# Second held part of the adjacency, a new order of the degree sums, and groups turned together with their sources

## The reference, cut to what matters

```python
# layer 0: two graph convolutions over the same matrix
A = adj + eye(n); d = rsqrt(A.sum(axis=1)); An = d[:, None] * A * d[None, :]
out = An @ (relu(An @ (x @ W1) + b1) @ W2) + b2
x = layernorm(x + out)
# layer 1: K = 2 heads of attention masked by (adj > 0) | eye
x_norm = ln(x, g1, b1)
h = x_norm @ ff0_w[i].T                      # for each head i
e = leaky_relu((h @ attn_w[i, :c])[:, None] + (h @ attn_w[i, c:])[None, :])
att = ln(softmax(where(mask, e, NEG), axis=1) @ h + x, g2, b2)
h_next += elu(att @ ff1_w[i].T) / K
x = layernorm(x + h_next)
```

## Time and profile before

| | us |
|---|---|
| median of 3 runs | 1012.15 (1011.77 to 1013.4) |
| the profiled execution | 1014.17 |
| its span, first to last instruction | 1011.5 |
| TensorE busy (matmuls) | 962.6 |
| VectorE busy | 729.5 |
| ScalarE busy | 485.6 |
| GpSimd busy | 231.9 |
| mean granted clock of TensorE | 0.985 |

### The profile page before, as it was taken

The page is one execution under the profiler, slowest core; times in us unless marked ns, Lnnn a source line. Parts: engine busy times, 40 slices in busy tenths (PEclk is TensorE's granted clock), DMA queues, the critical chain, the costliest instruction groups (busy, mean ns, idle before and its releaser), DMA issues. The chain is left out here.

```text
span 1011.5 us, 9279 instructions
## 1 busy us (share of the span) xinstructions
PE 962.6 (95%) x2491; PEld 455.4 (45%) x2492; DVE 729.5 (72%) x1289; ACT 485.6 (48%) x756; POOL 231.9 (23%) x226
## 2 busy tenths in 40 slices
PE   4888999999999999999999999999999999999993
PEld 3333344444644444444655454444444444444541
DVE  4977777765645434427878777888779899888977
ACT  3344433221200000000088768778677888978774
POOL 0322223233157000005600001000049501010013
PEclk9899999999999999999999999999999999999997
DMA  9999999999399999992322122223213233323211
GB/s 362 415 419 418 417 416 416 414 417 387 149 357 370 383 391 386 388 371 111 115 74 84 62 94 73 94 64 103 68 57 104 76 103 94 104 63 95 93 53 41
DMA packets 71378, 220.08 MB, mean 218 GB/s; under 512 B 5351, under 2 KB 44839, under 8 KB 61223
## 3 DMA queue, kind: packets, MB, share of 16 engines
q1 hardware_dynamic: 67360, 205.87, 54.1%
q10 hardware_dynamic: 3974, 13.73, 3.3%
HBM read 199.63 MB, written 19.96 MB: 217 GB/s over the span
## 5 line engine op out<-in xcount | busy, mean ns | idle before, releaser
L1502 PE MATMUL ps<-T,Yw 128*128 128x512 f32 x1024 | 444.5, 593 | 3.1 <-DVE T L1178 2.5
L1502 PE MATMUL ps<-colbuf,stat 128*128 128x512 f32 x800 | 349.2, 595 | 0.0
L1178 DVE SCALAR_TENSOR_TENSOR T<-T,mring 128x2048 f32<-128x2048 f32 x125 | 286.1, 2290 | 67.5 <-ACT T L692 66.6
L692 ACT ACTIVATE T<-Rrow,small,ratio 128x1024 f32<-128x1024 f32 x250 | 294.8, 1231 | 62.2 <-PE ps L1502 61.9
L1502 PEld LDWEIGHTS ps<-T,Yw 128*128 128x128 f32 x1024 | 194.0, 190 | 239.7 <-issue 231.7
L1502 PEld LDWEIGHTS ps<-colbuf,stat 128*128 128x128 f32 x800 | 152.5, 191 | 191.1 <-issue 190.9
L1008 DVE TENSOR_SCALAR mtile<-colbuf 128x4096 uint8<-128x4096 f32 x28 | 65.9, 2355 | 81.4 <-DMA mask<-mtile 81.4
L611 ACT ACTIVATE W<-W 128x1024 f32<-128x1024 f32 (+13 forms) x57 | 61.7, 1082 | 72.4 <-DMA W<-in_adj 71.5
L539 POOL TENSOR_SCALAR rs<-sumsq 128x4 f32<-128x4 f32 x14 | 15.9, 1138 | 309.7 <-ACT squares L739 309.7
L629 ACT ACTIVATE stat<-xw_g 128x128 f32 x20 | 6.2, 309 | 158.8 <-DVE mtile L1011 76.8
L485 POOL PARTITION_ALL_REDUCE Rrow<-W x32 | 36.1, 1127 | 164.2 <-DVE W L902 139.7
(11 more groups left out here) (203 smaller groups left out, 727.1 us busy)
## 6 DMA issues: line engine op xcount, KB each, us to landing
colbuf<-in_adjT SPq DMA_DIRECT2D x48, 1024.0 KB, 15.7
colbuf<-in_adjT SPq DMA_DIRECT2D x24, 2048.0 KB, 10.5
mring<-mask SPq DMA_DIRECT2D x128, 256.0 KB, 2.7
mask<-mtile ACTq DMA_DIRECT2D x26, 512.0 KB, 10.9
colbuf<-in_adjT SPq DMA_DIRECT2D x16, 768.0 KB, 15.5
W<-in_adjT SPq DMA_DIRECT2D x4, 2048.0 KB, 11.0
W<-in_adj SPq DMA_DIRECT2D x12, 512.0 KB, 12.3
Rrow<-s_src SPq DMA_DIRECT2D x9, 512.0 KB, 4.2
```

What stands on the lines that cost most here:

```text
L692: last = act.activation(T[:, c % TS, j, :], Rrow[:, g % 2, :], ACT.Relu, scale=ratio[:, c * JB + j:c * JB + j + 1], bias=small[:, 8:9])
L1178: v.scalar_tensor_tensor(out=tile, in0=tile, scalar=1.0, in1=mring[:, c % TS, :, :].rearrange("p b n -> p (b n)"), op0=ALU.add, op1=ALU.mu ...
L1502: return pe.matmul(*args, skip_group_check=True, **kw)
```

## The change

A second held part `side` (rows 4 to 15 of column blocks 4 and 5, 12 x 256 columns) lies in memory that is free at that time: the upper half of the row of 1/d and the buffer of source rows. It is loaded ahead of row 2. Rows 4 and 5 are then read from column 2048 on as well, and the column loads of blocks 4 to 15 leave out 256 columns more; TensorE's second group becomes two matmuls for them. Corner and side are summed by halving adds. The own sum of block b+1 is formed behind `diag` of block b, from tiles b-1 and b, and the long sum (now `scalar_tensor_tensor`) comes after it. The constant 1 of the diagonal goes into two later steps in place of L910. In the turn, groups 2 to 7 are multiplied by `turner`, the identity with the four source columns beside it, instead of being transposed; their last two blocks go into the bank of the group two before. Groups 0 and 1 keep the transposition and `sources`. ScalarE normalises and copies the source columns; GpSimd computes the combined scale `comb`; seven products z instead of eight stand ahead of the attention.

```diff
+    SB, SR = CB + 2, CR - CB
...
-        corner_part = Rrow[:, 0, 0:CB * P]
+        corner_part = Rrow[:, 1, 4 * P:8 * P]
+        side = [dinv_row[:, N // 2:N].rearrange("p (j n) -> p j n", j=CR // 2), Rrow[:, 0, :].rearrange("p (j n) -> p j n", j=CR // 4)]
+        side_part = Rrow[:, 1, 4 * P:6 * P]
...
         def row_parts(b):
 
-            from_block = CR if b < CB else b
+            from_block = CR if b < SB else b
...
             if b < CR:
-                return slice(CB * P, N // 2), slice(N // 2, N)
+                return slice((CB if b < CB else SB) * P, N // 2), slice(N // 2, N)
...
-        Z_FIRST, Z_BANKS, Z_WAITING = 4, 4, 8
+        Z_FIRST, Z_BANKS, Z_WAITING = 4, 3, 7
...
+                if b == 2:
+                    for part, landed, lo, hi in zip(side, side_loaded, (CB, CR - CB), (CR - CB, CR)):
+                        sp.dma_start(part, corner_cols[:, lo:hi, CB * P:SB * P]).then_inc(landed, 16)
...
+                if b == B // 2:
+                    pool.wait_ge(pe_block, COL_CREDIT + (CR - CB))
...
-                pool.tensor_tensor(rstd[:, group(k)], rstd[:, group(k)], half[:, group(k)], ALU.pow).then_inc(scale_ready, 1)
-
-            def scale_again(k):
-                pool.wait_ge(scale_ready, k + 1)
+                pstep(pool.tensor_tensor(rstd[:, group(k)], rstd[:, group(k)], half[:, group(k)], ALU.pow))
+                pool.wait_ge(means_ready, k + 1)
+                pool.tensor_tensor(shift[:, group(k)], neg_mean[:, group(k)], rstd[:, group(k)], ALU.mult).then_inc(scale_ready, 1)
+
+            def scale_both(k):
+
+                pool.wait_ge(moments_ready, k + 1)
                 own = group(k)
-                r = r2[:, own]
...
-
-            for k in range(NG):
+                r = comb[:, own]
+                pstep(pool.tensor_scalar(r, mv[:, own, 1], 1.0 + LN_EPS, 0.0, ALU.mult, ALU.add))
+                pstep(pool.tensor_tensor(r, r, eps_both[:, own], ALU.add))
+                pool.tensor_tensor(r, r, half[:, own], ALU.pow).then_inc(comb_ready, 1)
+
+            for k in range(NG - 1):
                 scale_rows(k)
-                scale_again(k)
+                scale_both(k)
+            scale_both(NG - 1)
+            scale_rows(NG - 1)
...
+            def copy_sources(k):
+                act.wait_ge(stats_ready, k + 1)
+                if k >= WHOLE:
+                    for i, at in enumerate((k, k - 2)):
+                        last = act.activation(raw_st[:, k * BPG + 2 * i:k * BPG + 2 * i + 2, :],
+                                              ps[:, at, 0:2 * TW].rearrange("p (b n) -> p b n", n=TW)[:, :, P:TW], ACT.Copy)
+                    last.then_inc(raw_st_ready, 1)
+
+            def copy_first_sources(k):
+                act.wait_ge(st_done, k + 1)
+                act.activation(raw_st[:, group(k), :], ps[:, k, OWN_ST:GW].rearrange("p (b m) -> p b m", m=2 * K), ACT.Copy)\
+                    .then_inc(raw_st_ready, 1)
+
+            def normalise(k):
+                act.wait_ge(scale_ready, k + 1)
+                for b in range(k * BPG, (k + 1) * BPG):
+                    last = act.activation(x1[:, b, :], turned(b), ACT.Identity, scale=rstd[:, b:b + 1], bias=shift[:, b:b + 1])
+                last.then_inc(x1_ready, 1)
+
+            for k in range(NG - 1):
...
+                copy_sources(k)
+                normalise(k)
+                if k < WHOLE:
+                    copy_first_sources(k)
+            copy_sources(NG - 1)
...
+            read_z(2)
+            normalise(NG - 1)
+            for r in range(3, Z_FIRST):
                 read_z(r)
...
+            def own_sums(b):
+
+                own = cols(b)
+                tiles = {CB: (b - 2, b - 1), CB + 1: (b - 2,)}.get(b, (b - 2, b - 1))
...
+                for n, tile in enumerate(tiles):
...
+                    v.tensor_tensor(colacc[:, own], colacc[:, own], colbuf[:, tile % RING, own], ALU.add)\
+                        .then_inc(own_step if b < SB or n == 0 else colown_done, 1)
+                if b < SB:
+                    v.wait_ge(own_step, steps + len(tiles))
+                    v.tensor_tensor(colacc[:, own], colacc[:, own], side_part[:, cols(b - CB)], ALU.add).then_inc(colown_done, 1)
+
             def add_rest(b):
 
-                before, rest = (b - 1) % RING, slice(max(b + 1, CB) * P, N)
-                if b < CB:
+                before, rest = (b - 1) % RING, slice(max(b + 2, CB) * P, N)
+                if b <= CB:
                     v.wait_ge(near_loaded[before], 16 * ((b - 1) // RING + 1))
                 if b <= HB2:
                     v.wait_ge(col_loaded[before], 16 * ((b - 1) // RING + 1))
                 if b == 1:
                     v.tensor_copy(colacc[:, rest], colbuf[:, before, rest]).then_inc(colacc_done, 1)
                 else:
-                    v.tensor_tensor(colacc[:, rest], colacc[:, rest], colbuf[:, before, rest], ALU.add).then_inc(colacc_done, 1)
-
-            def over_corner(out, rows, columns, done):
-                v.tensor_reduce(out, corner[:, rows, columns].rearrange("p j n -> p n j"), AX_X, ALU.add).then_inc(done, 1)
-
-            def corner_sums(b):
-
-                own = cols(b)
-                over_corner(colacc[:, own], slice(CR // CP, CR), own, corner_summed)
-                v.wait_ge(corner_summed, b + 2)
-                v.tensor_tensor(colacc[:, own], colacc[:, own], corner_part[:, own], ALU.add).then_inc(colown_done, 1)
+                    v.scalar_tensor_tensor(out=colacc[:, rest], in0=colbuf[:, before, rest], scalar=1.0, in1=colacc[:, rest],
+                                           op0=ALU.mult, op1=ALU.add).then_inc(colacc_done, 1)
+
+            CW = CB * P
+
+            def halve(scratch, k, out):
+
+                row0, wide = k * (CR // CP), CR // CP // 2
+                a = corner[:, row0:row0 + wide, :].rearrange("p j n -> p (j n)")
+                b = corner[:, row0 + wide:row0 + 2 * wide, :].rearrange("p j n -> p (j n)")
+                v.tensor_tensor(scratch[:, 0:4 * CW], a, b, ALU.add).then_inc(corner_summed, 1)
...
+                v.tensor_tensor(scratch[:, 0:2 * CW], scratch[:, 0:2 * CW], scratch[:, 2 * CW:4 * CW], ALU.add)\
+                    .then_inc(corner_summed, 1)
...
+                v.tensor_tensor(out, scratch[:, 0:CW], scratch[:, CW:2 * CW], ALU.add).then_inc(corner_summed, 1)
...
+
+            def side_sums():
+
+                scratch, wide = dinv_row[:, CB * P:CR * P], (SB - CB) * P
+                half = wide * (CR - CB) // 3
+                whole = side[0].rearrange("p j n -> p (j n)")
+                v.wait_ge(side_loaded[0], 16)
+                v.tensor_tensor(scratch[:, 0:half], whole[:, 0:half], whole[:, half:2 * half], ALU.add).then_inc(side_summed, 1)
+                v.wait_ge(side_loaded[1], 16)
+                v.wait_ge(side_summed, 1)
+                v.tensor_tensor(scratch[:, 0:half], scratch[:, 0:half], side[1].rearrange("p j n -> p (j n)"), ALU.add)\
+                    .then_inc(side_summed, 1)
...
-            over_corner(corner_part[:, :], slice(0, CR // CP), slice(0, CB * P), corner_summed)
+            halve(dinv_row[:, 0:N // 2], 0, corner_part)
             v.wait_ge(xw_done, NG)
             v.wait_ge(corner_loaded[1], 16)
-            corner_sums(0)
+            halve(colacc[:, N // 2:N], 1, colacc[:, 0:CW])
+            for b in range(CB):
+                v.tensor_tensor(colacc[:, cols(b)], colacc[:, cols(b)], corner_part[:, cols(b)], ALU.add).then_inc(colown_done, 1)
             for b in range(B):
                 u = b % RING
...
-                    v.wait_ge(colacc_done, b - 1)
-                    v.tensor_tensor(colacc[:, own], colacc[:, own], colbuf[:, before, own], ALU.add).then_inc(colown_done, 1)
-                elif b + 1 < CB:
-                    corner_sums(b + 1)
                 v.wait_ge(colrow_ready, b + 1)
                 v.tensor_tensor(colown[:, :], colrow[:, b % 2, :], ident[:, :], ALU.mult).then_inc(colpart_step, 1)
-                v.wait_ge(colpart_step, 3 * b + 1)
+                v.wait_ge(colpart_step, 2 * b + 1)
                 v.tensor_reduce(colpart[:, :], colown[:, :], AX_X, ALU.add).then_inc(colpart_step, 1)
-                v.wait_ge(colpart_step, 3 * b + 2)
-                v.tensor_scalar(colpart[:, :], colpart[:, :], 1.0, None, ALU.add).then_inc(colpart_step, 1)
-                if 1 <= b <= HB2:
-                    add_rest(b)
-                v.wait_ge(colpart_step, 3 * b + 3)
+                v.wait_ge(colpart_step, 2 * b + 2)
...
-                if HB2 < b < B - 1:
+                if b + 2 == CB:
+                    side_sums()
+                if CB <= b + 1 < B:
+                    own_sums(b + 1)
+                if 1 <= b < B - 2:
                     add_rest(b)
...
+                v.wait_ge(moments_ready, k + 1)
+                v.tensor_scalar(neg_mean[:, group(k)], mv[:, group(k), 0], -1.0, None, ALU.mult).then_inc(means_ready, 1)
...
+
```

(84 more changed lines are left out.)

131 lines of the change are left out of this document (69 added, 62 removed).

## The result

The changed kernel takes 1016.51 us (median of 7 runs, 1015.52 to 1018.34) against 1013.4 for the kernel before beside it (7 runs, 1011.77 to 1014.58): ratio 1.0036, 95% interval 1.0025 to 1.0048, so it is slower, by some 3.7 us, where 2.1 were forecast. Its profiled execution took 1015.83 us, span 1013.9.

The account below looks back on a forecast made before the run. VectorE's chain was taken as the degree stage's bound, DMA a close second, TensorE's work the turn's. Stage +3.7 and turn -1.6 gave +2.1 us: 1014.3 for the median, range 1003 to 1018.

Parts of the forecast that it names:

- part 1: Degree stage order: GpSimd's reduction, asked for just after the long sum begins, is blocked; 8.46 us a block, 0.1 more.
- once its reading is over, a sum doesn't hurt it: Degree stage: a reduction begun 0.54 us before long sum L876 still took 1.07 us.
- R1: Rival, degree stage: the reduction passes beside the long sum, blocks 7.0 us until DMA rules; 1004.5 us, chance 0.33.
- the pair L556 and L1178: GpSimd's L556 took 2.48 us (median 0.45) beside VectorE's three-operand L1178; taken as evidence that the reduction is blocked.
- part 2: Held columns, early blocks: 1.57 MB more up to row 3, 3.8 us at 418 GB/s; block 4 2.5 us late.
- The side adds: VectorE before block 3: four adds of 1024, 1024, 512 and 256 columns, 3.7 us with steps.
- the corner: Start of the degree stage: corner halved by adds, 4.3 us where L879 took 7.15; first `stat` within 0.5, taken as 0.
- The sum of the stage: Degree stage, blocked: 2.5 + 11 blocks x 0.08 + 0.3 for blocks 15 to 17 = +3.7 us; bounds +1.5 and +6.
- The turn: Turn of the groups: TensorE net -2.1, `highest` no longer waits, gref about 2.4 earlier; -1.6 us, bounds -2.5 and +2.
- R3: Rival, turn: bank waits on ScalarE stall TensorE two or three times by about 2.5 us; 1019.3 us, chance 0.10.
- R2: Rival: reduction blocked but early blocks cost nothing, stage even and the turn pays; 1010.5 us, chance 0.10.

Follow-up runs that it names:

- the first run: The changed kernel with the long sums written with two operands again: 1016.76 us, ratio 1.0036 to the kernel before.
- the turn alone: Degree stage of the kernel before, the rest as in the changed kernel, so only the turn is new: 1011.19 us, ratio 0.9984 to the kernel before.

## Why the prediction was nearly right

- *The mechanism, reduction blocked by the long sum* (part 1): right to 0.1 us. 8.46 us a block was forecast, 8.52 (blocks 4 to 5) and 8.46 (5 to 6) were measured; eleven blocks lose 0.7 where 11 x 0.08 = 0.9 was said. That three operands change nothing was shown by the first run. That "once its reading is over, a sum doesn't hurt it" holds for the row it was read from, but not for the copy of block 1: in the trace before, a reduction begun 0.54 us ahead of that copy (L874, 31.77) took 2.80 us.
- *R1* fell, and the reason given for keeping it high (the excluding rows are of other operations) was no reason: the pair L556 and L1178 was a good model. What R1 would have given is approached by moving the request: blocks of 6.9 to 7 us, then waits for tiles, 0.9938 to 0.9946 x 1012.15 = 1005.9 to 1006.7, against its 1004.5.
- *The early blocks* (part 2) are the step that was mis-sized: +2.5, measured +4.6. Row 2's second half was priced by bytes over 418 GB/s, at 39.7; it came to ScalarE at 41.79, `stat` 2 at 45.16 for 42.9, `stat` 3 at 55.95 for 53.5, block 4's at 64.93 for 62.5: one and the same 2.3 to 2.5 us carried on. Of the +4.6 the side part alone is 6.8 in this order (65.35 less 58.52 without it); the order gives 2.2 back. The late row is only in part explained. By its bytes the side part costs 3.8 us, as forecast; the lower rate from 32 to 40 us (377 for 410 GB/s, 0.26 MB) costs 0.6 more; some 1.4 of the 5.8 us stay open. SyncE's 12.33 us, which nobody had priced, come with it, but the trace doesn't show them as the cause, since the DMA engines moved as much during them as before. With the later loads row 2 is issued at 23.14 again and its first half is summed at 35.65 for 40.52, yet the end is only 1.4 us earlier, since VectorE then waits for the side part itself. The side adds were priced at 3.7 and took 3.9 (45.75 to 49.65); the corner cost 0.25 (first `stat` 28.53 against 28.28).
- *The sum of the stage*: +3.7, measured +5.5 = 4.6 + 0.7 + 0.2 behind block 15. Within the bounds named (+1.5 and +6).
- *The turn*: -1.6 forecast, and a ratio of 0.9984 to 1013.2 is -1.6. That the numbers agree is in part luck, for it did not come by the way told: gref comes 0.8 us earlier against the start of the turn, not 2.4. `highest` lost its wait, as said; yet `st` now waits 1.55 us for GpSimd's `comb` L563, and group 7 stands 0.78 us for VectorE's L1157, as the `sources` of group 0 do for ScalarE (0.80; 0.5 was said).

```profile
512.22 0.39 DVE L1194 TENSOR_TENSOR st<-diag,comb 128x128 f32<-128x128 f32 x1 [1.55 <-POOL comb L563]
...
514.00 0.22 DVE L1417 TENSOR_REDUCE highest<-ps 4x1 f32<-4x128 f32 x1
...
515.06 0.16 DVE L1421 COPY gref<-ps 128x1 f32<-128x1 f32 x1 [0.58 <-PE ps L1600]
```

  The rest came elsewhere: the turn itself 0.7, and the gap ahead of it, 1.81 us in the trace before, absent with the turn alone too. That gap ends with the landing of a tile of the second product and is 0 to 2.1 us in others of these traces (0.6, 1.1 and 1.7 among them), with the new turn too, so how much of the 1.6 belongs to the turn stays open; up to the first chunk the traces show 0.7.
- *R3*, the turn catching, did not come: no group of 2 to 6 waits. *R2* is half of it, the turn without the early loss.

## What to carry to other kernels

Where an operation of one engine stands for as long as another engine's operation runs, move its request beside short operations. Put 0.2 us behind the start of a 3.7 us sum it costs the whole sum, whether that sum is written with two operands or three (4.51 us for 1.07); beside one-column steps it took its 1.07 us.

Don't price a load that is moved ahead of others by its bytes at the common rate alone: here they said 3.8 us, and the row behind came 5.8 late. Read in the trace what rate such loads move at, and don't take the time that the issuing engine stands for time that the DMA loses: SyncE stood 12.33 us at 412 GB/s.

And try two limits together. The same side part cost 7.8 us while VectorE's chain was the bound (1016.5 against 1008.7), and gained 3.4 once the reduction no longer stood and the tiles' landing was (0.9962 against 0.9996).

## What was not expected of the hardware

- A pair of loads of 1 KB pieces (1 MB and 0.5 MB) held SyncE for 12.3 to 13.0 us in the second of them in every run that had the pair; parted, 7.40 us fell on the row load behind the first. The DMA engines moved 412 GB/s in the meantime (16.5 to 29 us), with and without the pair.
- Either use of GpSimd's cross-partition operation, reduction or spread, takes 4.51 us when it is started 0.2 us into a 3.75 us sum, 2.77 when it is started 0.18 us into a 2.02 us copy with one input, and 1.07 alone.
- TensorE's block 3 took 7.87 us for fourteen matmuls that take 6.17 in block 2. Its granted clock is 1.00 (2.4 GHz) from 35 to 57 us and 0.50 (1.2 GHz) from 58 to 60; before it fell the engine had stood 3.65 us and run for about one. It cost nothing here, as block 4 waited for its `stat` another 0.24.
